# Router logits as eight more columns of the score and value products, and a reordered run of expert pairs

## The reference

```python
x = x + tanh(g_xattn[0]) * _L0_xattn_ref(ctx_1024, _layernorm(x), wq, wk, wv)
#   Q = _layernorm(x) @ wq; K = ctx_1024 @ wk; V = ctx_1024 @ wv; softmax(Q @ K.T) @ V, per batch
x = x + tanh(g_ffn[0]) * _L0_ffn_ref(_layernorm(x), Wg, W1, W2, W3)
#   scores = xt @ Wg.T (8 experts); the top 2, weighted by their raw scores w
#   out_t = sum over the two experts of w * (silu(xt @ W1[e].T) * (xt @ W2[e].T)) @ W3[e].T
```

## Time and profile before

| | us |
|---|---|
| three runs | 603.81, 605.8, 606.28 (median 605.8) |
| profiled execution | 600.83 |
| its span, first to last instruction | 598.9 |
| busy in the span: PE, DVE, ACT, POOL | 570.4, 327.5, 329.6, 259.8 |
| steps, z of step 1 to z of step 15 on TensorE | 136.0 |
| from pair 0's gathered rows to the last up chunk of pair 7 | 103.7 |

### The profile page before, as it was taken

One profiled execution on the slowest core, in us unless ns is written; L12 is line 12 of the kernel. 1 busy time (PEld: TensorE's weight loads), 2 busy tenths in 40 slices (PEclk: granted clock), 3 DMA queues, 4 the chain that ended last, 5 costly groups with the idle time before them and its releaser, 6 DMA issues.

```text
span 598.9 us, 14784 instructions
## 1 busy us (share of the span) xinstructions
PE 570.4 (95%) x4765; PEld 502.4 (84%) x4765; DVE 327.5 (55%) x861; ACT 329.6 (55%) x473; POOL 259.8 (43%) x244
## 2 busy tenths in 40 slices
PE   5999999899899999989999999999999999999995
PEld 4787888788788889878898898898898899888783
DVE  3589788888878786864334334334334334333332
ACT  3887988789774554343444444434435435444442
POOL 4057374637347777633333333332332432433323
PEclk9999999999999999999999999999999999999998
DMA  7577687767523333442332332232322223223322
GB/s 247 188 228 240 194 252 257 236 192 225 156 75 104 84 76 87 112 122 43 47 65 38 47 59 45 46 55 48 47 49 53 43 49 59 38 37 46 58 35 26
DMA packets 52371, 61.50 MB, mean 103 GB/s; under 512 B 7632, under 2 KB 46160, under 8 KB 52304
## 3 DMA queue, kind: packets, MB, share of 16 engines
q1 hardware_dynamic: 34656, 38.15, 21.3%
q0 software_dynamic: 13296, 18.23, 17.9%
q10 hardware_dynamic: 4352, 4.20, 2.0%
HBM read 36.90 MB, written 23.66 MB: 101 GB/s over the span
## 4 chain that ended last, share of the span: by engine, by line
PE 79%; DVE 8%; DMA 4%; issue 3%; ACT 3%; SPq 1%; POOL 1%; POOLq 0%; ACTq 0%; DVEq 0%; another core or an unknown queue 0%
PE psum L927 36%; PE psum L959 21%; PE psum L802 10%; PE psum L936 4%; PE psum L856 3%; DMA w_in<-in_W3T 2%; PE psum L795 2%; PE psum L840 2%; DMA w_in<-in_W1T 1%; DVE w_lo L1061 1%; PE psum L945 1%; ACT w_hi L675 1%; DVE w_lo L1068 1%; DVE xa L1139 1%; DVE mask L1172 1%
## 5 line engine op out<-in xcount | busy, mean ns | idle before, releaser
L599 POOL DMA_INDIRECT out<-w_in,id_s x71 | 128.4, 1809 | 234.8 <-ACT w_in L750 121.7
L927 PE MATMUL psum<-arena,w_hi 128*128 128x256 f16 x1408 | 211.3, 273 | 1.1 <-issue 1.0
L927 PEld LDWEIGHTS psum<-arena,w_hi 128*128 x1408 | 137.0, 98 | 17.3 <-issue 1.4
L927 PE MATMUL psum<-arena,w_lo 128*128 128x256 f16 x704 | 134.4, 273 | 0.0
L682 ACT ACTIVATE arena<-psum 128x1024 f16<-128x1024 f16 (+1 forms) x39 | 36.9, 947 | 97.5 <-PE psum L856 88.8
L567 POOL DMA_INDIRECT rows_by_expert<-xn2r,slot_i x64 | 74.8, 1168 | 25.2 <-issue 20.8
L1352 DVE SCALAR_TENSOR_TENSOR arena<-psum,h_unit,arena 128x1280 f32<-128x1280 f32 x32 | 49.6, 1550 | 63.7 <-PE psum L927 63.7
L927 PEld LDWEIGHTS psum<-arena,w_lo 128*128 x704 | 68.9, 98 | 8.0
L802 PE MATMUL psum<-arena 128*128 128x256 f32 x256 | 63.9, 394 | 1.1 <-ACT arena L690 0.3
L726 ACT ACTIVATE arena<-psum,w_unscale 64x256 f32<-64x256 f32 x32 | 15.0, 468 | 88.3 <-PE psum L927 86.2
L959 PE MATMUL psum<-w_hi,arena 128*128 x396 | 59.4, 273 | 2.1 <-issue 1.1
(11 more groups left out here) (182 smaller groups left out, 883.7 us busy)
## 6 DMA issues: line engine op xcount, KB each, us to landing
xa<-rows_by_expert SPq DMA_DIRECT2D x71, 136.0 KB
w_in<-in_W1T SPq DMA_DIRECT2D x8, 704.0 KB
w_in<-in_W3T SPq DMA_DIRECT2D x8, 640.0 KB
...
out<-w_in,id_s POOLq DMA_INDIRECT x71, 4.5
```

The costliest lines, as they stand in the source:

```text
L599: pool.indirect_dma_start(out=out[:, :], out_offset=bass.IndirectOffsetOnAxis(ap=id_s[:, t8:t8 + 1], axis=0), in_=y_s[:, t8 % 4, :], in_of ...
L927: ins = pe.matmul(flat_ps[:, j * N2:(j + 1) * N2], w12[w_part][:, c, bass.ds(e * (2 * H) + j * P, P)], xg_t[:, k, x_part, c, :], start=(q ...
```

## The change

The router weights become eight more columns of two operands. In step 0 TensorE transposes wv (`wvt_ps`), VectorE copies it, TensorE multiplies it by the centred router weights (`wvg_ps`), and ScalarE copies that behind wv (`wv_s` is 264 columns wide); the router weights themselves stand behind z (`z_s`). The scores product (x times z) then gives x's part of the logits, the value product (probabilities times v) the attention's part, and `residual` adds the two for every batch (`logits`). The transposes of finished rows, their copy and the router product are gone for all sixteen batches. The products v, scores and values have 264 columns, PSUM banks are shared out anew (one bank for each half of scores, v and values; rank, count and sum of squares share bank 7 with the second half of the values), so the second half of the values waits for VectorE's reads of the sums and the places. `rank` moves ahead of the scores.

In the pairs, batch m's high rows, choice, rank and slots all stand in its own pair (pair 0: rank and slots late in the pair), VectorE takes over the low rows behind `low`, and `other_slots` runs behind `low` of pair 5. `full_pairs` moves ahead of step 14's `lo12`. SyncE's first loads are reordered. Cut to its core:

```diff
...
+        pt_ps = bank[0].rearrange("p (t s) -> p t s", t=KT)
...
+        v_ps = psum[:, 2:4, 0:D + E]
+        sc_ps = psum[:, 4:6, 0:S]
+        xw_ps = psum[:, 4:6, S:S + E]
+        sc_and_xw_ps = psum[:, 4:6, 0:S + E]
+        last_pt_ps = bank[5].rearrange("p (t s) -> p t s", t=KT)
+        o_ps = psum[:, 6:8, 0:D + E]
...
             load_ctx(0)
+            sp.dma_start(wg_s[:], WgT.rearrange("(c p) e -> p c e", p=P)).then_inc(s_wg_in, 16)
             load_x(0)
...
-            sp.dma_start(wv_s[:], wv.rearrange("(c p) d -> p c d", p=P)).then_inc(s_w, 16)
-            load_x(1)
-            sp.dma_start(wg_s[:], WgT.rearrange("(c p) e -> p c e", p=P)).then_inc(s_w, 16)
+            sp.dma_start(wv_s[:, :, 0:D], wv.rearrange("(c p) d -> p c d", p=P)).then_inc(s_w, 16)
+            load_w12(0)
             with nc.allow_non_contiguous_dma(reason="one gate to every partition"):
                 sp.dma_start(gates[:, 0:1], g_xattn.rearrange("(a n) -> a n", a=1).to_broadcast([P, 1])).then_inc(s_gate, 16)
                 sp.dma_start(gates[:, 1:2], g_ffn.rearrange("(a n) -> a n", a=1).to_broadcast([P, 1])).then_inc(s_gate, 16)
-            load_w12(0)
+            load_w12(1)
+            load_x(1)
             load_ctx(1)
+            load_w3(0)
             load_x(2)
 
             sp.wait_ge(s_const, CONSTS)
             sp.dma_start(out[T:T + P, :], zrow[:, 0:D]).then_inc(s_dummy, 16)
 
             load_x(3)
-            load_w3(0)
-            load_w12(1)
...
-                if i in AT_PAIR:
-                    low_rows(AT_PAIR[i])
...
+                    if n == 0:
+                        act.wait_ge(s_wvg, 1)
+                        act.activation(wv_s[:, :, D:D + E], wvg_ps, ACT.Copy).then_inc(s_wvg_copied, 1)
...
-                if n in AT_STEP:
-                    copy_rows(AT_STEP[n])
...
+                at_least(pe, s_place, m)
...
-                product(o_ps, probs_t, v_s[:, m % 2]).then_inc(s_pv, 1)
...
-            def turn_rows(m, to=t2_ps):
-                pe.wait_ge(s_x2, m + 1)
-                at_least(pe, s_t2_copied, m)
-                turn(to, xa[:, x_at(m):x_at(m) + KT, :], KT, KD).then_inc(s_t2, 1)
...
-            def router(m):
...
-                for t in range(KT):
-                    for c in range(KD):
-                        ins = pe.matmul(rt_ps[:, t * E:(t + 1) * E], x2_t[:, c, t * P:(t + 1) * P], wg_c[:, c, :],
-                                        start=(c == 0), stop=(c == KD - 1))
-                ins.then_inc(s_rt, 1)
...
+                product(o_ps, probs_t, v_s[:, m % 2], tiles=(0,))
+
+                pe.wait_ge(s_half, min(m + 2, B))
+                if m in AT_STEP:
+                    pe.wait_ge(s_place, AT_STEP[m] + 1)
+                if m + 1 == COUNT_STEP:
+                    pe.wait_ge(s_plan, 1)
+                product(o_ps, probs_t, v_s[:, m % 2], tiles=(1,)).then_inc(s_pv, 1)
...
+                at_least(pe, s_x2, u - 1)
...
+            turn_x(0)
+            pe.wait_ge(s_w, 16)
+            turn(wvt_ps, wv_s, KD, KD).then_inc(s_wvt, 1)
...
-                if n in AT_STEP:
-                    turn_rows(AT_STEP[n])
+                    pe.wait_ge(s_qk_copied, 1)
+                pe.wait_ge(s_ctx[k], 16 * (n // 2) + 16)
+                at_least(pe, s_z_copied, n)
+                product(z_ps, qk, ctx_s[:, k]).then_inc(s_z, 1)
+                if n == 0:
+
+                    pe.wait_ge(s_wvt_copied, 1)
+                    pe.wait_ge(s_wg, 1)
+                    for i in range(KD):
+                        for c in range(KD):
+                            ins = pe.matmul(wvg_ps[:, i, :], wv_t[:, c, i * P:(i + 1) * P], wg_c[:, c, :],
+                                            start=(c == 0), stop=(c == KD - 1))
+                    ins.then_inc(s_wvg, 1)
+                    pe.wait_ge(s_wvg_copied, 1)
+                at_least(pe, s_v_copied, n)
+                product(v_ps, ctx_s[:, k], wv_s).then_inc(s_v, 1)
+                pe.wait_ge(s_t1_copied, n + 1)
                 if live(n - 1):
                     turn_probs(n - 1)
-                if live(n):
-                    weight_sum(n)
-                    pe.wait_ge(s_z_copied, n + 1)
-                    pe.wait_ge(s_t1_copied, n + 1)
-                    product(sc_ps, x_t, z_s).then_inc(s_sc, 1)
-                if n in AT_STEP:
-                    router(AT_STEP[n])
-                if live(n):
-                    pe.wait_ge(s_half, n + 1)
                 if n - 1 in AT_STEP:
+                    pe.wait_ge(s_x2, n - 1)
                     rank(AT_STEP[n - 1])
                 if n == COUNT_STEP:
                     count(COUNTED)
+                weight_sum(n)
+                pe.wait_ge(s_z_copied, n + 1)
+                at_least(pe, s_exp, n)
+                at_least(pe, s_xw, n)
+                product(sc_and_xw_ps, x_t, z_s).then_inc(s_sc, 1)
                 if n == B - 1:
-                    pe.wait_ge(s_t1_copied, B)
+                    pe.wait_ge(s_pt_copied, B - 1)
                     turn_gathered(0, 0, 0)
                 if live(n - 1):
                     values(n - 1)
                 if live(n + 1):
-                    m = n + 1
-                    pe.wait_ge(s_x[m % RING], 16 * (m // RING) + 16)
-                    at_least(pe, s_t1_copied, m)
-                    turn(t1_ps, xa[:, x_at(m):x_at(m) + KT, :], KT, KD).then_inc(s_t1, 1)
-
+                    turn_x(n + 1)
 
             pe.wait_ge(s_map, 1)
 
...
+                            pe.wait_ge(s_x2, B - 1)
+                            rank(IN_STEPS - 1)
...
-                if at == 0:
-                    rank(IN_STEPS - 1)
-                if at - 1 in AT_PAIR and at > 0:
-                    rank(AT_PAIR[at - 1])
-                    if AT_PAIR[at - 1] == B - 1:
+                if at in AT_PAIR and at > 0:
+                    rank(AT_PAIR[at])
+                    if AT_PAIR[at] == B - 1:
                         count(B)
                 if on(i):
                     at_least(pe, s_hmul, i)
-                    if at == 0:
-                        to_hidden(range(KH, KM - 1), expert[u], k)
-                        pe.wait_ge(s_x2, B)
-                        to_hidden(range(KM - 1, KM), expert[u], k).then_inc(s_u, 1)
-                    elif pair(i):
+                    if pair(i):
                         to_hidden(range(KH, KM), expert[u], k).then_inc(s_u, 1)
                     else:
                         for b in range(2):
                             ins = to_hidden_rows(u1_ps[:, b, :], H + b * HB, HB, expert[u], k)
                         ins.then_inc(s_u, 1)
-                    if at in AT_PAIR:
-                        pe.wait_ge(s_silu, i + 1)
-                        turn_rows(AT_PAIR[at], x10_ps)
                 if i >= 0 and on(i + 1):
                     at_least(pe, s_silu, i + 1)
                     turn_gathered(i + 1, (i + 1) // 2, 1 - k)
+                if at == 0:
+                    pe.wait_ge(s_x2, B)
+                    rank(AT_PAIR[0])
                 if on(i - 1):
                     if at == 1:
                         pe.wait_ge(s_lo3, E)
                     to_output(i - 1, (k4 - 1) % 4, 0, expert[u - 1])
-                if at in AT_PAIR:
-                    router(AT_PAIR[at])
                 if on(i) and not pair(i):
                     turn_hidden(i)
             over_slots(pe, moe_step, take)
...
+            def rest_of_rows(m):
+
+                r = m % ROWS
+                dve.wait_ge(s_xf, m + 1)
+                dve.wait_ge(s_xh, m + 1)
+                dve.tensor_copy(xn2r[:, r, :, ID_AT].bitcast(I32), token[:, KT * m:KT * m + KT])
+                dve.tensor_tensor(xn2r[:, r, :, D // 2:D].bitcast(F16), xn2f,
+                                  xn2r[:, r, :, 0:D // 2].bitcast(F16), ALU.subtract).then_inc(s_xn2, 1)
...
                 dve.tensor_reduce(nmax[:], sc_ps, AX_X, ALU.max, negate=True).then_inc(s_raw, 1)
+                dve.tensor_copy(x_logits[:, m % 2], xw_ps).then_inc(s_xw, 1)
...
                 dve.wait_ge(s_pv, m + 1)
                 for t in range(KT):
+                    dve.scalar_tensor_tensor(out=logits[:, m, t, :], in0=o_ps[:, t, D:D + E], scalar=rsum[:, t:t + 1],
+                                             in1=x_logits[:, m % 2, t, :], op0=ALU.mult, op1=ALU.add)
                     x2 = xa[:, x_at(m) + t, :]
-                    ins = dve.scalar_tensor_tensor(out=x2, in0=o_ps[:, t, :], scalar=rsum[:, t:t + 1], in1=x2,
+                    ins = dve.scalar_tensor_tensor(out=x2, in0=o_ps[:, t, 0:D], scalar=rsum[:, t:t + 1], in1=x2,
                                                    op0=ALU.mult, op1=ALU.add)
                 ins.then_inc(s_x2, 1)
...
+                if n == -1:
                     centre_router()
+                    dve.wait_ge(s_wvt, 1)
+                    dve.tensor_copy(wv_t, wvt_ps).then_inc(s_wvt_copied, 1)
...
+                if n == COUNT_STEP + 1:
```

(30 more changed lines are left out.)

102 lines of the change are left out of this document (39 added, 63 removed).

## The result

The changed kernel took 607.25 us (median of 16 runs, 604.46 to 610.63), the kernel before 605.73 us (16 runs, 601.26 to 609.95): a ratio of 1.0039, 95% interval 1.002 to 1.0058. Three more sets of the same pair, on the chips of the experiments, gave 1.0004 (0.9968 to 1.0041), 1.0014 (0.9985 to 1.0042) and 1.0036 (1.0009 to 1.0063). The change costs 0 to 0.4%, at most some 2 us; two of the four intervals include no change. The forecast was 4.5 us the other way; 607.25 us lies near the slow end of its range of 594 to 608.

A forecast was written before the change was run, and what follows sets the result against it. TensorE bounds from pair 8 on; a W3-load, ScalarE and VectorE loop paces the steps. Terms -2.7 + 1.1 + 0.3 - 1.7 + 4.3 + 1.5 - 2.1 - 5.2 = -4.5 us: 596.3 profiled, 601.3 median, range 594 to 608.

The forecast's parts named there:

- The start: First microseconds: W1 asked for sooner, v of step 0 waits for a four-engine chain; +0.3 us, bounds -1 and +1.5.
- The clock: TensorE's clock halves after waits: +1.5 us counted in pair 1 only; by the rule short waits might cost, left out.
- The steps: Sixteen steps before the pairs: -2.7 us from TensorE, +1.1 from VectorE's added operations in seven steps; -1.6 us.
- The reading of the loop: In the steps, W3 load, ScalarE and VectorE form a loop of 19.73 us per two steps, without router product.
- Rival A: TensorE sets the pace in the steps: they give -11 us, in all -13.9, 591.9 us; chance 0.15.
- Rival C: VectorE bounds every step, its three added operations cost 0.75 us each step: in all +6.4, 612.2 us; chance 0.15.
- Hand-over: From steps to pairs: plan ahead of lo12 comes 1.7 us earlier, so do pair 0's rows; -1.7 us, bounds -2.5 and 0.
- Pairs 0 and 1: TensorE waits over 5 us before rank(11) in pair 1: +4.3 us, plus +1.5 for the slow clock behind it.
- Pairs 2 to 5: VectorE's loop takes 12.75 us a pair, TensorE waits 1.3 in each: -2.1 us, bounds -6.2 and +2.
- Pairs 6 and 7: other_slots begins earlier, so both pairs take 22.7 us instead of 27.96: -5.2 us, bounds -5.2 and -2.
- so the cover holds: Pairs 6 and 7: the output product waiting for the copy behind combined(6) stands one microsecond after that copy.
- Rival B: Plans gain nothing: TensorE waits in pair 7 as before, pair 0's rows wait for SyncE; -1.4 or less, 604.5; chance 0.20.

The follow-up runs named there:

- a_start2: Second run of the a_start kernel, nothing else changed: 602.05 us, ratio 0.9945 to the kernel before.
- a_again3: Unchanged copy of the changed kernel: 606.25 us, ratio 1.0036 to the kernel before.
- a_x_first: Changed kernel with x of steps 1, 2, 3 loaded ahead of W1, W2, W3 again, as before: 604.37 us, ratio 0.9986.
- a_warm: Changed kernel with three useless matmuls on TensorE ahead of the sum of squares in each odd step: 602.09 us, ratio 0.9955.
- a_start: Changed kernel with the old load order and ScalarE copying z and the router's columns of wv ahead of the first W1's squares: 598.08 us, ratio 0.9910.
- a_sum_late: Changed kernel with TensorE's product for the sum of squares moved behind the scores product: 609.33 us, ratio 1.0096.
- a_plan_late: Changed kernel with the plan of the first pairs behind the low parts of step 14 again: 609.51 us, ratio 1.0087.
- a_choice_first: Changed kernel with a batch's choice in the pairs ahead of the next batch's moments and its own high rows on VectorE: 600.46 us, ratio 0.9937.
- a_slots_back: Changed kernel with the later pairs' plan (other_slots) in front of combined(5), no longer behind low(5): 606.55 us, ratio 1.0078.
- a_rows_pool: Changed kernel with the low rows of the pairs back on GpSimd instead of VectorE: 605.87 us, ratio 1.0021.

## Why the prediction was wrong

**The start** is the step that failed, +0.3 forecast against +4.8 in the profiles and 4.2 by the time of `a_start2` beside `a_again3`. The forecast named two mechanisms, that W1 comes sooner and that `v` waits for a chain over four engines, and set them against each other. It left out what the diff shows plainly: W2 passes the second x and W3 the third, 640 KB each, and these x stand ahead of the scale in VectorE's queue. For the plans it asked what now stands ahead of them in the queue, for the loads it did not. Its bound of +1.5 was too small as well. Either cost alone is enough: with the old order of loads alone `lo3` of step 1 still ends at 37.0 (`a_x_first`), with both undone at 34.1 and 34.4.

**The clock** is the second. The forecast quoted the rule against the change and then left it out of all but one wait, since short waits in the trace of before had no slow stretch behind them. But those waits were 1.2 us at most; the fold made new ones of up to 2.4. `a_warm` puts the price of the slow stretches in start and steps at 3.0 us, most of it in the steps.

**The steps**: -1.6 forecast, -1.4 measured. That the numbers meet is luck. With the clock full the twelve steps take 112.4 (`a_warm`) and 113.7 us (`a_start`), 4.2 and 2.9 under before, and the slow stretches take the difference back. The forecast's own term for VectorE does not follow either: 0.4 us in seven steps is 2.8, not 1.1. The reading of the loop was right: VectorE's waits for `rank` are gone, TensorE is 4.7 to 7.5 us less busy (105.5 and, in `a_start` with a full clock, 102.6, where it was 110.2), and the twelve steps are 1.4 us shorter. Rival A, TensorE as the bound, would have shown 8.7 us a step; they take 9.6. Rival C did not come: in the twelve steps VectorE's busy time rose by 1.1 us, not by 12 x 0.75. That ScalarE's order is a bound too (`a_sum_late`) it did not see.

**Hand-over**: -1.7 forecast, -2.3 measured, 3.3 by `a_plan_late`. Right; before, a half-clock stretch stood behind the longer wait, and it is gone with it, which may be the rest.

**Pairs 0 and 1**: +5.8 with the clock, +5.0 measured. The wait of about 5 us before `rank` and the stretch at 0.50 are those foretold (4.60 us in `a_start`; 2.50 and 2.37 where the copy is late), and by `a_choice_first` 1.6 us of it is the choice behind the other parts (2.37 against 0.74).

**Pairs 2 to 5**: -2.1 forecast, -0.1 measured. Where no late signal shows (`a_start`, `a_sum_late`, `a_slots_back`) they take 49.4 us, -2.9, and TensorE waits 0.90 us in each of three pairs, where 1.3 was forecast. The mechanism was right, by `a_rows_pool`; the late signal, which the forecast could not know, goes with the loss of that gain. Its cause stays open.

**Pairs 6 and 7**: -5.2 forecast, -2.8 measured. Right in kind by `a_slots_back`, mis-sized: the step "so the cover holds" looked at the copy behind `combined` and not at the rows of pair 8, which account for a third to a half of it (0.40 to 1.14 us). Rival B had named the loss, for another reason.

Without the start the forecast's terms sum to -4.8 and the measured ones to -1.1. The difference is in pairs 2 to 5 (2.0 us) and in pairs 6 and 7 (2.4); the other stages nearly cancel.
